# Side work on TensorE behind the second pair of scores, and one stack of loads behind four stores, in a fused attention and experts kernel

## What is computed

```python
q = layernorm(x) @ Wq.T            # split into 16 heads, scaled by 256 ** -0.5
k = ctx @ Wk.T;  v = ctx @ Wv.T
attn = softmax(q k^T, axis=queries)
attn = attn / sum(attn, axis=context)
x = x + tanh(g_xattn) * (attn v) @ Wo.T
xn = layernorm(x)
probs = softmax(xn @ router_w.T);  top 2, weights made to sum to 1
x = x + tanh(g_ffn) * sum over the top 2 of weight * (gelu(xn @ w1[e]) @ w2[e])
```

## Time and profile before

| | us |
|---|---|
| median of three runs | 1816.68 |
| the profiled execution | 1814.16 |
| its span, first to last instruction | 1812.4 |
| exponentials of batch 0, from 30.6 | 157.4 |
| batches 1 to 6, each | 152.6 |
| batch 7, to 1245.0 | 141.3 |

### The profile page before, as it was taken

One profiled execution on the slowest core, in us unless ns is written; L12 is line 12 of the kernel. 1 busy time (PEld: TensorE's weight loads), 2 busy tenths in 40 slices (PEclk: granted clock), 3 DMA queues, 4 the chain that ended last, 5 costly groups with the idle time before them and its releaser, 6 DMA issues.

```text
span 1812.4 us, 31594 instructions
## 1 busy us (share of the span) xinstructions
PE 1683.1 (93%) x9980; PEld 900.1 (50%) x9980; DVE 1419.2 (78%) x2293; ACT 1283.9 (71%) x3640; POOL 542.7 (30%) x825
## 2 busy tenths in 40 slices
PE   8989999999999989999999998887799999999997
PEld 5223233333333323333333332214799999999997
DVE  7979999999999999999999999997444444444442
ACT  5989999999999999999999999995111111111111
POOL 3331251352244225235223422213222222222222
PEclk9999999999999999999999999999899999999999
DMA  8547215613711731461272163419222222222221
GB/s 233 129 112 189 63 51 148 162 40 96 196 53 52 176 108 47 133 181 40 75 194 60 58 162 83 148 54 299 86 35 38 36 37 35 38 35 38 35 36 28
DMA packets 128245, 172.87 MB, mean 95 GB/s; under 512 B 14496, under 2 KB 105760, under 8 KB 128128
## 3 DMA queue, kind: packets, MB, share of 16 engines
q1 hardware_dynamic: 113152, 150.51, 30.3%
q0 software_dynamic: 14144, 20.44, 6.5%
q10 hardware_dynamic: 832, 0.53, 0.1%
HBM read 117.96 MB, written 53.47 MB: 95 GB/s over the span
## 4 chain that ended last, share of the span: by engine, by line
PE 36%; ACT 29%; DVE 20%; issue 7%; POOL 3%; DMA 3%; SPq 1%; POOLq 0%; DVEq 0%; ACTq 0%
ACT w_all L899 27%; DVE negmax L1080 14%; PE scores L1474 13%; PE scores L1487 13%; PE scores L716 3%; PE acc L729 3%; POOL routed_rows L1273 1%; DVE resid L975 1%; ACT w_all L857 1%; DMA out<-row_t,gate_token 1%; PE spare L579 1%; PE spare L573 1%; PE spare L1464 1%; DVE rz L1066 1%; SPq L389 1%
## 5 line engine op out<-in xcount | busy, mean ns | idle before, releaser
L899 ACT ACTIVATE w_all<-scores,negmax 128x512 f32<-128x512 f32 (+1 forms) x1664 | 1127.8, 751 | 24.8 <-DVE negmax L1080 19.3
L1080 DVE TENSOR_REDUCE negmax<-scores 128x2 f32<-128x1024 f32 (+1 forms) x832 | 1002.2, 1216 | 65.6 <-PE scores L716 59.2
L716 PE MATMUL scores<-q_stack,w_all 128*128 128x512 bf16 (+1 forms) x1664 | 501.9, 383 | 50.0 <-ACT w_all L899 48.3
L899 ACT ACTIVATION_READ_ACCUMULATOR w_all<-scores,negmax 128x1 f32 (+1 forms) x1664 | 449.3, 270 | 0.0
L729 PE MATMUL acc<-w_all,vz 128*32 128x512 f32 (+1 forms) x3328 | 443.7, 605 | 3.0 <-POOL vz L1296 2.8
L1515 ACT ACTIVATE projections<-scores 128x512 f32<-128x512 f32 x142 | 84.9, 598 | 449.0 <-PE scores L1474 449.0
L716 PEld LDWEIGHTS scores<-q_stack,w_all 128*128 128x128 bf16 (+1 forms) x1664 | 115.7, 99 | 524.9 <-ACT w_all L899 395.5
L1296 POOL TENSOR_TENSOR vz<-w_all,rz 128x68 f32<-128x68 f32 (+1 forms) x416 | 124.7, 300 | 789.3 <-DVE rz L1066 763.7
L1474 PEld LDWEIGHTS scores<-row_t,q_stack 128*128 128x128 f32 x2272 | 265.9, 193 | 7.6 <-issue 2.8
L1474 PE MATMUL scores<-row_t,q_stack 128*128 128x128 f32 x2272 | 267.5, 276 | 2.0 <-DVE row_t L1542 1.8
L1487 PE MATMUL scores<-room,projections 128*128 128x256 f32 x1136 | 256.8, 379 | 0.0
(11 more groups left out here) (208 smaller groups left out, 1027.8 us busy)
## 6 DMA issues: line engine op xcount, KB each, us to landing
w_all<-k_parts SPq DMA_DIRECT2D x248, 200.1 KB, 3.5
w_all<-in_w SPq DMA_DIRECT2D x16, 1024.0 KB, 10.8
q_stack<-q_parts SPq DMA_DIRECT2D x248, 64.0 KB, 3.4
k_parts<-parts SPq DMA_DIRECT2D x42, 300.0 KB, 2.9
w_all<-in_ctx_t SPq DMA_DIRECT2D x7, 1601.0 KB, 7.3
parts<-routed SPq DMA_DIRECT2D x71, 129.0 KB, 2.1
q_parts<-parts SPq DMA_DIRECT2D x14, 384.0 KB, 3.2
routed<-pad_row SPq DMA_DIRECT2D x8, 645.0 KB, 9.5
```

Of the source, the lines that this page charges most:

```text
L716: mm = pe.matmul(scores[0:r, 2 * (u % SLOTS) + j % 2, :], k_stacks[g][:, j, lt * P:lt * P + r], q_stack[:, g, j, :], start=True, stop=True)
L899: e = act.activation(probs[0:r, s % RING, j, :], scores[0:r, 2 * (u % SLOTS) + j % 2, :], ACT.Exp, bias=negmax[0:r, u % 4, j % 2:j % 2 + 1 ...
L1080: dve.tensor_reduce(negmax[0:r, u % 4, :], scores[0:r, 2 * (u % SLOTS):2 * (u % SLOTS) + 2, :], AX.X, ALU.max, negate=True).then_inc(negma ...
```

## The change

Three edits. On SP, in the first batch, the 16 loads of group 3's stack go from between the fourth and the fifth K store to behind the eighth. On TensorE a step's order becomes: first scores, second half of a piece if there is one, second scores, then what begins a piece (a first half or a whole piece), `first_logits`, `weigh`. On VectorE all pieces but `out_proj` are taken at the end of p = 1.

```diff
@@ sync, run
-            if b == 0:
-                load_stacks(0, 3)
             if it.tail:
                 sp.wait_ge(fill_taken, it.made("out_proj", 1))
                 sp.dma_start(out_rows[b - 1], x2[:, :, :]).then_inc(x2_stored, 16)
             if it.next:
                 for c in ORDER[KCHUNK:2 * KCHUNK]:
                     store_parts(it, c)
+            if b == 0:
+                load_stacks(0, 3)
@@ tensor, run
                 if it.cur:
                     unit_scores(it.b, s, 0)
                 for f, halves in it.halves(s):
-                    fill(it, *f, halves)
+                    if halves == (1,):
+                        fill(it, *f, halves)
+                if it.cur:
+                    unit_scores(it.b, s, 1)
+                for f, halves in it.halves(s):
+                    if halves != (1,):
+                        fill(it, *f, halves)
                 if it.tail and s == LOGITS - 1:
                     first_logits(it)
-                if it.cur:
-                    unit_scores(it.b, s, 1)
@@ vector, run
-                    if f and f[0] not in ("v", "own_v", "x_turn") and p == (f[0] in ("q", "k")):
+                    if f and f[0] not in ("v", "own_v", "x_turn") and p == (f[0] != "out_proj"):
                         take(it, *f)
```

## The result

The changed kernel takes 1828.86 us, the median of four runs (1827.97 to 1830.58), against 1815.24 (1813.56 to 1817.67) of the kernel before, now also of four. The ratio is 1.0077, with a 95% interval of 1.0061 to 1.0093: slower by 13.6 us, where 8.1 was predicted. The profiled execution took 1829.36, with a span (first to last instruction) of 1827.6, 15.2 longer than before's 1812.4.

The account below looks back on a forecast made before the run. ScalarE was taken as the bound, with VectorE and TensorE close behind. 11.4 (middle batches) + 0.9 (last) + 1.4 (first) - 5.6 (stack) = +8.1 us on the 1816.68 median: 1824.8 us, range 1809 to 1834.

Parts of the forecast that it names:

- six middle batches: Batches 1 to 6: side pieces behind the second scores cost +1.9 us each, +11.4 in all.
- stack: First batch, SP: moving the 16 loads ends ScalarE's wait for the fifth K store, -5.6 us (-4.7 to -6.0).
- Rival (d): First batch: the take still waits for a store, so 5.6 us isn't won; 1830 us; 5 per cent.
- Rival (a): Gaps close as second scores come sooner and slack absorbs the pieces: 1803 to 1811 us; 20 per cent.
- Rival (b): Side-work costs of 0.1 to 1.3 us a batch cancel against the stack: 1813 to 1820.3 us; 22 per cent.
- the ledger's first entry: Middle batch, steps 0 to 3: 0.6 us lost behind k 0, then won back, leaving 0 at step 4.
- F - 0.1 and F: Delay of next first scores by a piece of length F ahead of value matmuls; F - 0.1 was taken.
- pairs of v: Two halves of v in successive steps: exponentials due at X + 7.17 against ScalarE's 7.11, 0.06 us each.
- v 6: Unhalved last v piece: ScalarE's copy, ahead of its step's exponentials, waits for it; 0.35 to 0.5 us.
- Rival (c): Pieces cost F in full and stalls add up: 3.2 us a batch, +18, 1834.5 us; 10 per cent at or above.
- The second exponentials gain what the next first lose: VectorE: copies of turns, logits and prefix move behind the second maximum and behind rz, with no work added.
- There is no term for the clock: TensorE: granted clock 1.00 in the middle batch, pauses stay about 1 us, so no clock cost was counted.

Follow-up runs that it names:

- stack_only: Kernel before with only the SP edit (fourth stack's 16 loads behind the eighth K store): 1809.01 us, ratio 0.9968.
- warm: Changed kernel plus 5 and 6 idle transposes on TensorE between scores in steps 1 and 2 of batch 0: 1827.86 us, ratio 1.0067.
- halves_only: Kernel before with the SP edit and every first half, only these, behind the second scores; VectorE's order as before: 1828.19 us, ratio 1.0065.
- waiting_fewer: Kernel before with the SP edit and only first halves of steps 2, 12, 14, 34 (first batch 12, 14, 34) behind second scores: 1801.18 us, ratio 0.993.

## Why the prediction was right or wrong

**Direction and range: right.** 1828.86 lies between 1809 and 1834, among the slower cases, which had 0.59.

The terms of the sum against the profiled executions (the stack as in stack_only, the side work of batch 0 as warm, 152.88, less stack_only, 151.64):

| term, us | predicted | measured |
|---|---|---|
| six middle batches | +11.4 | +14.3 |
| batch 7 | +0.9 | +1.5 |
| side work of batch 0 | +1.4 | +1.2 |
| stack | -5.6 | -5.7 |
| clock in step 2 of batch 0 | 0 | +1.6 |
| first exponential, and behind the batches | 0 | +0.2, +2.0 |
| sum, of the profiled spans | +8.1 | +15.2 |

**The stack: right**, to 0.1 us alone (-5.7 for -5.6), though 0.8 of it stands in step 25, and is probably the clock's and not VectorE's. The Trainium skill (DMA: Bandwidth & Descriptors, Issuing engines are not separate DMA queues) calls the sequencer's time to start a DMA usually small relative to the DMA itself. That agrees for a single load here: 0.64 us on SP, against a median of 3.2 to 3.4 from issue to landing. But 16 in a row, 10 us, held back a store, and their place alone was worth 5.7 us. Rival (d) falls.

**The mechanism: right.** First halves behind the second scores make the next first scores late (halves_only: +2.3 a batch). Rival (a), that gaps close and nothing is lost, needed less than 0.7 us a batch and falls for the change as made. What is true in it is small and stands in waiting_fewer: where a half had waited for VectorE, moving it wins 1.1 us a batch. Rival (b), with its at most 1.3 a batch, falls too. (The lower end of (b) doesn't follow from its costs: 0.1 us in each of seven batches, less 5.6, gives 1811.8 and not 1813. Nothing rests on it.)

**The size of a middle batch: +1.9 for +2.38. Two steps of its walk through the batch were off.**

| against before, at step | 4 | 8 | 12 | 17 | 23 | 31 | 32 | 35 | 39 | 41 | 45 | 47 | 51 |
|---|---|---|---|---|---|---|---|---|---|---|---|---|---|
| predicted | 0 | .54 | .6 | .2 | .45 | .65 | 1.1 | .3 | .6 | .9 | 1.05 | 1.6 | 1.9 |
| measured | .43 | .82 | 1.00 | .57 | .83 | 1.03 | 1.45 | .76 | 1.08 | 1.59 | 1.82 | 2.22 | 2.39 |

The first is the ledger's first entry, "0.6 is lost in steps 0 and 1 behind k 0 and won back in 2 and 3". Measured: 0.67 lost, 0.24 won back. Step 2 took 3.28 us in before, and ScalarE's own pace with a copy of k is 3.05, so 0.23 was all that it could win, however long TensorE's wait for L975 had been. So at step 4 the batch stood 0.43 above the forecast, and it stayed 0.3 to 0.5 above it up to step 39.

The second is the choice between F - 0.1 and F, where no row stood. Four matmuls of 256 columns take 0.96 ahead of value matmuls (512.56 to 513.52 in after) against 0.86 ahead of scores, two of 400 columns 0.77 (525.20 to 525.97 in waiting_fewer) against 0.67. So a piece behind the second scores costs about 0.1 more than its old spacing, which with the 0.54 shrunk to 0.44 is F in full. It shows in the pairs of v: each was put at 0.06, and steps 36 and 37 lose 0.27, 43 and 44 lose 0.22. With F in full the 0.06 becomes 0.16; the rest wasn't taken apart. By step 45 the batch stood 0.77 above the forecast, and 0.28 of that came back by step 51.

The later entries have the right places: step 14's gap closed (-0.30 measured in that step), q's wait (+0.42, then -0.69), take_acc in step 40 (+0.41 for 0.3). v 6 cost 0.37, inside its 0.35 to 0.5, though 0.14 of it came back in step 48, which the forecast left out. Rival (c) had F in full right and the total, 3.2 a batch, too high by 0.8; which of its stalls are less than counted wasn't taken apart.

**"The second exponentials gain what the next first lose", and no cost for VectorE's order: wrong**, though the sum hardly shows it. VectorE's edit costs 3.9 us where TensorE's isn't made, and gives 1.9 back where it is. The forecast counted the copy's length, which doesn't change, and not who waits for it, except at attn_turn. So out_proj 0 was put down to its own place, and moving it back made the batch slower. That the sum came near all the same is partly luck: with both orders changed the cost of VectorE's is mostly given back, and the forecast had it at nothing.

**"There is no term for the clock": wrong** for batch 0, right for the middle batches (1.00 in both). I had judged it by the length of TensorE's pauses in a middle batch and not looked at steps 0 to 2 of the first, where pauses of 0.73 and 1.22 us now follow one another. Where the clock fell there, it cost 1.6 us.

**The signs to look for:** ScalarE's wait for maxima rose to 3.9, just under the 4 to 5 forecast. The value matmuls stand 0.44 + 0.96 = 1.40 behind the second scores where a half of 256 columns is begun, for 1.3. Steps 23 and 25 of batch 0 take 3.05, for 3.04. The last batch loses its 1.5 in steps 6, 7, 9, 21, 22, 38 and 40, and nothing where the other batches lose by pieces of v.

## What to carry to other kernels

A piece of side work that is moved out of one wait, on an engine that works in order, lands ahead of what is queued next: work out the slack of the new neighbour, and credit a wait that goes only with what the bounding engine itself had lost in that step. Move a piece only where its old place really waits (here four first halves, -1.1 us a batch), not all pieces of a kind; and let the engine that empties a buffer and the one that fills it keep matching orders, since either edit alone cost 4 us a batch. On a queue that issues both loads and stores, put the store that someone waits for ahead of loads that are needed much later (here more than 20 us after the last was issued, even in their new place).

## What the runs showed of the hardware

- A piece's spacing depends on what follows: four fp32 matmuls of 256 columns took 0.86 us to the next scores (bf16, 512 columns) and 0.95 to 0.96 to the value matmuls (fp32, 32 by 512).
- The granted clock went to 1.2 GHz in the first batch right behind TensorE pauses of no more than 0.73 and 1.22 us, in four of seven executions with these pauses; with the pauses cut to 0.18 and 0.56 it stayed at 2.4, in one execution. The same step at the lower clock took 1.6 us longer.
- Behind a wait of 4.6 us (TensorE, first batch, before) it went to 1.2 GHz too (0.57 in the mean of 106 to 110 us), and step 25, behind the wait, took 4.02 us instead of the 3.25 of stack_only, which has neither the wait nor the lower clock.
- In the last 567 us the code is the same in all kernels, and the stretch differs by up to 4.5 us (565.2 to 569.8); of the two whose clock is shown above the longer has the lower mean clock.
- ScalarE's instructions in a row overlap, so its busy time rose by 0.9 us a batch with no work added. From 515.54 to 516.42, 0.22 of the 0.88 is stall, and the profile's row prints no idle time ahead of the second.
